# Feed-forward of a hybrid block: squares and rotations bank by bank, the output projection one step later, the token shift as whole rows

## What is computed

```python
h = shift_token(x)                    # second half of each row comes from the row before
q, k, v = split(h @ wqkv)             # 128 -> 3 x 512, 8 heads of 64
q, k = rotary_xpos(l2norm(q) * qs, l2norm(k) * ks)
o = local_attention(q, k, v)          # window 64, keys: own window and the one before
x = x + o @ wo                        # 512 -> 128
h = layernorm(shift_token(x)) * lg + lb
a, g = split(h @ w1 + b1)             # 2 x 341
x = x + (a * gelu(g)) @ w2 + b2
```

## Time and profile before

| | us |
|---|---|
| median of 3 runs | 5035.15 |
| lowest, highest | 5034.42, 5037.8 |
| the profiled execution | 5039.37 |
| its span | 5037.7 |

### The profile page before, as it was taken

How to read it: one execution, slowest core, us unless ns; L and a number is a source line. 1 busy time by engine, 2 the same in 40 slices (tenths; PEclk the granted TensorE clock), 3 DMA queues, 4 the chain that set the end, 5 groups by cost and what they waited for, 6 DMA issues and landing times.

```text
span 5037.7 us, 101534 instructions
## 1 busy us (share of the span) xinstructions
PE 3958.2 (79%) x31924; PEld 2425.0 (48%) x31924; DVE 2871.0 (57%) x5889; ACT 2620.8 (52%) x6422; POOL 1703.7 (34%) x1415
## 2 busy tenths in 40 slices
PE   2999999996688888744666664999999917888886
PEld 1555555553455555522222222777777715555554
DVE  2555555555566676543444443666666656767664
ACT  1555555553566666423333332666666605666664
POOL 0000000000777777523222221111111128777773
PEclk9999999998899999865555555999999959999998
DMA  3222222221101101017999999777777611111111
GB/s 122 78 79 82 78 79 78 84 77 45 44 22 23 24 23 23 16 66 287 382 381 378 381 379 370 260 243 273 242 275 243 227 34 26 23 23 23 23 24 28
DMA packets 373723, 701.02 MB, mean 139 GB/s; under 512 B 53220, under 2 KB 160056, under 8 KB 373608
## 3 DMA queue, kind: packets, MB, share of 16 engines
q1 hardware_dynamic: 329576, 565.25, 32.8%
q0 software_dynamic: 44032, 134.30, 7.3%
HBM read 336.53 MB, written 314.64 MB: 129 GB/s over the span
## 4 chain that ended last, share of the span: by engine, by line
PE 60%; DMA 13%; DVE 7%; issue 7%; POOL 5%; ACT 3%; SPq 1%; DVEq 1%; POOLq 0%; ACTq 0%
DMA rel_k<-b_stage_k 12%; PE ps L332 5%; PE ps L1452 5%; PE ps L340 5%; PE ps L351 5%; PE ps L1461 5%; PE ps L862 4%; PE ps L1443 3%; PE ps L821 3%; PE ps L1472 3%; PE ps L882 2%; PE ps L836 2%; PE ps L847 2%; POOL f_rn L759 2%; PE ps L1344 2%
## 5 line engine op out<-in xcount | busy, mean ns | idle before, releaser
L1368 DVE COPY b_stage_k<-ps 128x640 f32<-128x640 f32 (+2 forms) x512 | 359.3, 722 | 471.1 <-DMA rel_k<-b_stage_k 412.3
L430 ACT ACTIVATE a_p<-a_s,a_min 128x512 f32<-128x512 f32 x512 | 367.1, 718 | 469.6 <-DVE a_min L474 469.6
L1365 ACT ACTIVATE b_stage_q<-ps 128x640 f32<-128x640 f32 (+2 forms) x512 | 316.4, 624 | 506.8 <-PE ps L1347 390.2
L474 DVE CUSTOM_DVE_ANT_0 a_s<-ps,a_table 128x512 f32<-128x512 f32 x512 | 333.5, 689 | 374.4 <-PE ps L332 371.8
L1526 ACT ACTIVATE c_p<-c_s,c_min 128x512 f32<-128x512 f32 x512 | 371.0, 725 | 291.9 <-PE ps L1461 179.8
L1344 PE MATMUL ps<-b_e,b_st_k 48*128 48x512 bf16 (+1 forms) x512 | 305.9, 597 | 263.8 <-DVE b_stage_k L1368 263.8
L1561 DVE CUSTOM_DVE_ANT_0 c_s<-ps,c_rq 128x512 f32<-128x512 f32 x512 | 353.2, 690 | 202.5 <-PE ps L1452 189.8
L188 POOL COPY y<-ln_rows 128x512 f32 x32 | 19.9, 621 | 1305.2 <-DVE ln_rows L180 1305.2
L757 POOL TENSOR_TENSOR f_rot<-f_rc,f_rs 128x1024 f32<-128x1024 f32 x128 | 302.9, 2367 | 354.3 <-DVE f_rs L1017 354.0
L942 ACT ACTIVATE f_p<-f_s,f_min 128x128 f32<-128x128 f32 x1024 | 397.6, 392 | 39.6 <-DVE f_min L1005 35.6
L759 POOL TENSOR_TENSOR f_rn<-f_ss,f_power 128x16 f32<-128x16 f32 x128 | 373.8, 2920 | 14.3 <-DVE f_ss L1026 0.4
(11 more groups left out here) (171 smaller groups left out, 9374.7 us busy)
## 6 DMA issues: line engine op xcount, KB each, us to landing
rel_q<-b_stage_q SPq DMA_DIRECT2D x64, 1280.0 KB, 7.7
rel_k<-b_stage_k SPq DMA_DIRECT2D x64, 1280.0 KB, 7.7
c_rq<-rel_q SPq DMA_DIRECT2D x64, 1024.0 KB, 7.3
c_rk<-rel_k POOLq DMA_DIRECT2D x64, 1024.0 KB, 11.8
a_table<-skew_bias SPq DMA_DIRECT2D x64, 896.0 KB, 4.6
f_vb<-f_v SPq DMA_DIRECT2D x256, 128.0 KB, 2.3
rel_k<-b_stage_k SPq DMA_DIRECT2D x32, 1024.0 KB, 9.4
rel_q<-b_stage_q SPq DMA_DIRECT2D x32, 1024.0 KB, 5.3
```

Source lines behind the costliest of these rows:

```text
L430: nc.scalar.activation(a_p[:, lt % 2, h, :], a_s[:, lt % 2, h, :], ACT.Exp, bias=a_min[:, lt % 2, h:h + 1], scale=-1.0, accum_out=a_sum[:, ...
L1368: moves_b1(dve, 1, lambda out, src: nc.vector.tensor_copy(out, src))
```

## The change

A fifth tile, `d`, four steps behind, enters every `step`. The output projection and the residual add are of `d`, at the start of the next step, in the MIXED bank; `mix_values` waits for that add. `Square` and the rotations go bank by bank with semaphores that count twice and six times a tile. At m=2 the first four exponentials stand behind the copies. At m=3 SP shifts whole rows of `y` (four tiles of 128 numbers, 2 KB a partition) into `f_h`, behind the residual add of `d`, and ahead of its `f_vb` transfers; VectorE then writes the left halves over (they are not shifted), and the statistics follow behind the reciprocal. The bias add on POOL moves from m=0 to m=1. Cut to its core:

```diff
 # sync_ffn
+            if m == 3 and ln is not None:
+                half = slice(DIM // 2, DIM)
+                hold(sp, f_x_mid, upto(d.g))
+                hold(sp, f_hn_ready, upto_b(ln.g - 1, LT))
+                rows = y[:, bass.ts(ln.y, LT), :]
+                sp.dma_start(f_h[1:P, :, :], rows[0:P - 1, :, :]).then_inc(f_shift_loaded, 16)
+                sp.dma_start(f_h[0:1, 1:LT, half], rows[P - 1:P, 0:LT - 1, half]).then_inc(f_shift_loaded, 16)
...
-            if m == 2 and ln is not None:
-                sp.dma_start(f_h[1:P, :, half], rows[0:P - 1, :, :]).then_inc(f_shift_loaded, 16)
...
 # pool_ffn
                 tt(f_rstd[:, :], f_lv[:, :], f_power[:, 0:LT], ALU.pow).then_inc(f_rstd_ready, 1)
-                hold(pool, f_shift_loaded, 32 * (mlp.g + 2))
+            if m == 1 and mlp is not None:
                 hold(pool, f_h_left, upto_b(mlp.g))
...
-            if m == 3 and ln is not None:
-                nc.gpsimd.tensor_copy(f_h[:, :, 0:DIM // 2], y[:, bass.ts(ln.y, LT), 0:DIM // 2]).then_inc(f_h_left, 1)
 # tensor_ffn
-            mm(ps[:, QK, :], h, f_wqkv[:, a.layer, 0:INNER], start=True, stop=True)
+            mm(ps[:, QK, :], h, f_wqkv[:, a.layer, 0:INNER], start=True, stop=True).then_inc(f_qk_full, 1)
 # transpose_qk, for k in (q, k)
+                if a is not None:
+                    pe.wait_ge(f_squared, upto(a.g - 1, 2) + k + 1)
+                    pe.wait_ge(f_turned, upto(a.g - 1, 6) + 3 * k + 3)
 # mix_values
-            pe.wait_ge(f_oT_moved, upto(c.g - 1))
+            pe.wait_ge(f_x_mid, upto(c.g - 1))
 # join_heads(m, d, mlp)
+            if m == 0 and mlp is not None:
+                pe.wait_ge(f_y_done, upto_b(mlp.g - 1))
+            if m == 1 and mlp is not None:
+                pe.wait_ge(f_hnT_moved, upto_b(mlp.g))
+            if m == 2 and mlp is not None:
+                pe.wait_ge(f_gelued, upto_b(mlp.g, 3))
+            if m == 3 and mlp is not None:
+                pe.wait_ge(f_hid_ready, upto_b(mlp.g, 3))
-                last = mm(ps[:, V_BANK, 0:DIM], f_oT[:, i * P:(i + 1) * P], f_wo[:, c.layer, i, :],
+                last = mm(ps[:, MIXED, 0:DIM], f_oT[:, i * P:(i + 1) * P], f_wo[:, d.layer, i, :],
 # new: ahead of turn_normed, chunk 2 of mlp_up and mlp_down
+        def mixed_free(c, d):
+            if c is not None:
+                pe.wait_ge(f_oT_moved, upto(c.g))
+            elif d is not None:
+                pe.wait_ge(f_x_mid, upto(d.g))
 # step of PE: behind project_v, ahead of transpose_probs
+            if d is not None:
+                join_heads(m, d, mlp)
-            if c is not None:
-                join_heads(a, c)
 # scalar_ffn
-                nc.scalar.activation(f_sq[:, :], ps[:, QK:QK + 2, :].rearrange("p b n -> p (b n)"),
-                                     ACT.Square).then_inc(f_squared, 1)
+                for k in range(2):
+                    act.wait_ge(f_qk_full, upto(a.g - 1, 2) + k + 1)
+                    nc.scalar.activation(f_sq[:, k * INNER:(k + 1) * INNER], ps[:, QK + k, :],
+                                         ACT.Square).then_inc(f_squared, 1)
-            if s2 is not None:
+            if s2 is not None and m != 2:
                 exps(s2, 0)
 # behind the copies f_pT, f_qT, f_kT, ahead of f_oT
+            if s2 is not None and m == 2:
+                exps(s2, 0)
 # vector_ffn: turn_heads, for k in (q, k): one rc of 512, two rs of 256
+                dve.wait_ge(f_squared, upto(a.g - 1, 2) + k + 1)
+                tt(rc, heads, cs[:, 0, k, :].unsqueeze(1).broadcast_to([P, HF, DF]), ALU.mult).then_inc(f_turned, 1)
 # statistics: first
+            hold(dve, f_shift_loaded, 32 * (ln.g + 2))
+            nc.vector.tensor_copy(f_h[:, :, 0:DIM // 2], y[:, bass.ts(ln.y, LT), 0:DIM // 2]).then_inc(f_h_left, 1)
 # step of DVE: behind the copy f_pT, ahead of sum_squares
+            if d is not None:
+                dve.wait_ge(f_out_full, upto(d.g))
+                tt(y[:, d.t, :], y[:, d.t, :], ps[:, MIXED, 0:DIM], ALU.add).then_inc(f_x_mid, 1)
 # statistics(ln) now behind the reciprocal
```

More of the change, by code:

```diff
@@ L654, in body @@
             for m in range(LT):
-                step(m, rows(0, m), rows(1, m), rows(2, m), rows(3, m), whole(-1), whole(-2), whole(1))
+                step(m, rows(0, m), rows(1, m), rows(2, m), rows(3, m), rows(4, m), whole(-1), whole(-2), whole(1))
         body(0, 0)
@@ L692, in sync_ffn, with step @@
         sp.wait_ge(f_zeros, F_ZEROS * (call + 1))
-        def step(m, a, b, s2, c, ln, mlp, nxt):
+        def step(m, a, b, s2, c, d, ln, mlp, nxt):
+            if m == 3 and ln is not None:
[5 more added lines that the diff above has]
+                sp.dma_start(f_h[0:1, 1:LT, half], rows[P - 1:P, 0:LT - 1, half]).then_inc(f_shift_loaded, 16)
             if a is not None:
@@ L700, in step @@
                 sp.dma_start(f_vb[0:WINDOW, (m + 1) % LT, :], f_v[WINDOW:P, m, :]).then_inc(f_vb_loaded[m], 16)
-            if m == 2 and ln is not None:
[L702 to L705, removed]
-                sp.dma_start(f_h[1:P, :, half], rows[0:P - 1, :, :]).then_inc(f_shift_loaded, 16)
-                sp.dma_start(f_h[0:1, 1:LT, half], rows[P - 1:P, 0:LT - 1, :]).then_inc(f_shift_loaded, 16)
         ffn_loop(sp, call, step)
@@ L749, in step @@
                 fetch(nxt)
-            if m == 3 and ln is not None:
-                hold(pool, f_x_mid, upto(ln.g * LT + 3))
-                hold(pool, f_hn_ready, upto_b(ln.g - 1, LT))
-                nc.gpsimd.tensor_copy(f_h[:, :, 0:DIM // 2], y[:, bass.ts(ln.y, LT), 0:DIM // 2]).then_inc(f_h_left, 1)
             if a is not None:
-                pool.wait_ge(f_turned, upto(a.g, 3))
+                pool.wait_ge(f_turned, upto(a.g, 6))
                 pool.wait_ge(f_normed, upto(a.g - 1))
@@ L780, in project_qk @@
             if b is not None and s2 is None:
[L781 to L782 removed]
+                pe.wait_ge(f_squared, upto(b.g, 2))
+                pe.wait_ge(f_turned, upto(b.g, 6))
             pe.wait_ge(f_qT_moved, upto(a.g - 2))
             pe.wait_ge(f_kT_moved, upto(a.g - 2))
[L785 removed]
+            mm(ps[:, QK, :], h, f_wqkv[:, a.layer, 0:INNER], start=True, stop=True).then_inc(f_qk_full, 1)
             mm(ps[:, QK + 1, :], h, f_wqkv[:, a.layer, INNER:2 * INNER], start=True, stop=True).then_inc(f_qk_full, 1)
         def project_v(a, h):
[L789 to L791 removed]
+            pe.wait_ge(f_v_moved, upto(a.g - 1))
             mm(ps[:, V_BANK, :], h, f_wqkv[:, a.layer, 2 * INNER:3 * INNER], start=True, stop=True).then_inc(f_v_full, 1)
@@ L826, in transpose_qk @@
         def transpose_qk(a, b):
[L827 to L832, removed]
-            pe.wait_ge(f_normed, upto(b.g))
-            for k, full in enumerate((f_qT_full, f_kT_full)):
+            pe.wait_ge(f_normed, upto(b.g))
+            for k, (full, moved) in enumerate(((f_qT_full, f_qT_moved), (f_kT_full, f_kT_moved))):
+                if a is not None:
+                    pe.wait_ge(f_squared, upto(a.g - 1, 2) + k + 1)
+                    pe.wait_ge(f_turned, upto(a.g - 1, 6) + 3 * k + 3)
+                else:
+                    pe.wait_ge(moved, upto(b.g - 1))
                 for i in range(PAIRS_F):
@@ L1010, in turn_heads @@
             dve.wait_ge(f_rotated, upto(a.g - 1))
[L1011 to L1018, removed]
+            for k in range(2):
+                heads = ps[:, QK + k, :].rearrange("p (h d) -> p h d", d=DF)
+                rc = f_rc[:, k * INNER:(k + 1) * INNER].rearrange("p (h d) -> p h d", d=DF)
+                rs = f_rs[:, k * INNER:(k + 1) * INNER].rearrange("p (h d) -> p h d", d=DF)
+                dve.wait_ge(f_squared, upto(a.g - 1, 2) + k + 1)
+                tt(rc, heads, cs[:, 0, k, :].unsqueeze(1).broadcast_to([P, HF, DF]), ALU.mult).then_inc(f_turned, 1)
+                for h in range(2):
+                    to, src = slice(h * 32, h * 32 + 32), slice((1 - h) * 32, (1 - h) * 32 + 32)
+                    tt(rs[:, :, to], heads[:, :, src],
+                       cs[:, 1, k, to].unsqueeze(1).broadcast_to([P, HF, 32]), ALU.mult).then_inc(f_turned, 1)
         def sum_squares(a):
@@ L1060, in step @@
                 normalize(mlp)
-            if m == 3 and ln is not None:
-                statistics(ln)
             if s2 is not None:
@@ L1066, in step @@
                 nc.vector.reciprocal(f_rsum[:, s2.par, :], f_sum[:, s2.par, :]).then_inc(f_inverted, 1)
-            if c is not None:
-                dve.wait_ge(f_out_full, upto(c.g))
-                tt(y[:, c.t, :], y[:, c.t, :], ps[:, V_BANK, 0:DIM], ALU.add).then_inc(f_x_mid, 1)
+            if m == 3 and ln is not None:
+                statistics(ln)
             if m == 2 and mlp is not None:
```

34 lines of the change are left out of this document (13 added, 21 removed).

## The result

The changed kernel is slower: median 5218.38 us (5216.2 to 5219.62, 4 runs) against 5034.88 (5034.42 to 5037.8), ratio 1.0363, 95% interval 1.0345 to 1.0381. I had forecast 4906, with a range to 4988, and gave "slower" 7 in 100. The page of the profiled execution (5216.2 us) now gives the token shift 7% of the chain that ended last (followed back from the last instruction, at each step to what released it).

The account below looks back on a forecast made before the run. No engine was full, so a cycle of waits was taken as the bound. Intervals of 9.5, 12.0, 13.4 and 13.0 made 47.95 us a batch, saving 109, plus 7 and 14: 130 less, forecast 4906 us, range 4868 to 4988.

Parts of the forecast that it names:

- landing of the shift: At m=3, whole-row data expected at R3+4.5, R3 being the end of m=3's rotations on VectorE; statistics then just covered.
- interval from m=3 to m=0: From the end of m=3's rotations to m=0's: 13.0 us forecast with the low clock charged, 14.8 before.
- third rival: The shift's second transfer keeps its long issue (6.90): batch 2.0 us longer, 5084 us; chance 0.07, shared with other slower mechanisms.
- ends of the calls: Token shift without cover at each call's end gets 7 us shorter: 14 us over two calls.
- seven tiles at the start of each: First seven tiles of each call gain half of 0.97 us a tile: 7 us together, bounds 0 and 14.
- R0 to R1: End of m=0's rotations on VectorE to end of m=1's: 9.5 us forecast, 10.1 before.
- R1 to R2: End of m=1's rotations to end of m=2's: 12.0 us forecast, 12.6 before; square behind Gelu.
- R2 to R3: End of m=2's rotations to end of m=3's: 13.4 us forecast, 14.0 before; reordering gives nothing, the late projection pays.
- The low clock: After m=3, PE's slow clock charged as today: 13.0 us to m=0, against 12.0 at full clock.
- full-clock case: Rival without low clock after m=3: 12.0 us to m=0 in place of 13.0, 4878 us; chance 0.13.
- Squares and rotations by bank: Each tile: VectorE works 0.14 us more, but the first rotation needs only the first bank's squares, about 1.3 earlier.
- The copy held by POOL: Rival at m=3: left-half copy waits for GpSimd's `f_qk`, batch 50.0 us, 4961 us; chance 0.30, shared with half the gain.

Follow-up runs that it names:

- a_split: The changed kernel with the shift of 127 partitions sent as two transfers, of 112 and 15 partitions: 4919.08 us, ratio 0.9767 to the kernel before.
- a_split_exps: The changed kernel with the shift as 112 + 15 partitions and the first four exponentials of m=2 back ahead of the copies: 4894.86 us, ratio 0.9721.
- lv_pool: `a_split_exps` with the addition of eps to the variance (`f_lv`) done by GpSimd, not VectorE: 4883.09 us, ratio 0.9703.
- a_whole: `a_split_exps` with `Square` and rotations over both banks again: 4898.19 us, ratio 0.9732.
- b_bank: `b_split` with squares and rotations bank by bank and nothing else of the change: 5066.78 us, ratio 1.0067.
- b_split: The kernel before the change, with its half-row shift sent as 112 + 15 partitions in place of 127: 5018.9 us, ratio 0.9969.

## Why the prediction was wrong

- **The step that failed is the landing of the shift.** "127 pieces of 2 KB are nearer to `f_vb`'s 64" took the size of a piece for what counts, and the 6.90 of the second issue for the price of 508 pieces. `f_vb` moves 64 partitions, a number with 16 as a divisor; the shift moves 127. R3+4.5 was R3+15, and with it the interval from m=3 to m=0 was 22.6 and not 13.0. My third rival had the place and the sign, but its ground was the issue (it was to decide at 5 us; the issue was 3.9, in five batches 0.7, and the landing late all the same), and its price of 2.0 a batch was 5.6. The sign that it gave was luck. The trace before had what was needed: between 1503 and 1511 the shift's 127 KB ran at 13 GB/s, 0.06 of the 16 engines' time (the window 1503.10 to 1511.00). I looked at issue and landing and not at the DMA share of that window.
- **The rest of the sum held for the batch, not for its two small terms.** With the shift as 112 + 15, which lands about where I had assumed (R3+4.8), a batch of `a_split` takes 48.25 in the first call and 48.78 in the second (13.0, 10.5, 10.6, 13.7, in some batches 14 to 15 for the first) where I had 47.95. In its profiled execution (4932 us; the median is 4919) the batches give 98 of the 109 us that I had. The ends of the calls give 9.5 of 14. The seven tiles at the start of each give nothing of 7: I had put half the gain of a full tile there with no row behind it.
- *R0 to R1 and R1 to R2* were 9.5 and 12.0 in the forecast; by the ends of the rotations after, 9.9 and 11.3 in the batch above, 9.6 and 11.5 at the median. The square did come right behind Gelu, which took 1.84 and not 2.07: before, the third Gelu had started 0.2 late, behind TensorE's product, though I had read the three as without a gap. `f_rot` was 0.75 late in m=1, not 1.3.
- *R2 to R3*: reciprocal at R2+6.5 (6.4 forecast), 13.7 for 13.4. "The reordering itself gives nothing" was too kind to it: it costs 24 us (`a_split_exps`).
- *The low clock* that I charged in m=3 is gone with the shift as 112 + 15 (0.99 over 460 us). So 13.0 from m=3 to m=0 came out right by luck: the charge for the clock, 1.0, was wrong, and two things that I had not charged took its place. `f_lv` was held by GpSimd (without that, in `lv_pool`, it is 12.5), and TensorE's last product let the add to `y` start at R3+6.9 in `lv_pool` and not at the R3+6.4 of my full-clock case.
- *Squares and rotations by bank*: of no effect on the sum (`a_whole`), and a loss of 48 us without the late projection (`b_bank`). The gain comes from the output projection's new place and the order that goes with it: from `b_split`'s 5019 to `a_whole`'s 4898. No run takes the projection's place apart from the later shift and statistics.
- *The copy held by POOL* was a rival at its right size (15.0 from m=3 to m=0), in 9 of 32 batches of `a_split` instead of all.

## What to carry to other kernels

Before a transfer is judged by its bytes or pieces, look at the DMA share of the window in which it is alone: 0.06 means one engine of 16, and then the number of partitions on the slowest dimension is the first thing to change (112 + 15 in place of 127). A transfer that is badly spread costs nothing while it starts early; moving it later by a step can put most of its length on the path (10.0 of 13.8 us here), so its length must be measured and explained first, not inferred from a relative. And a shorter wait can cost more than it gives where it lengthens another one before TensorE (2.04 to 2.50 in `b_bank`): look at the granted clock of the next tiles.

## What the runs showed of the hardware

- SBUF to SBUF, at the share of one DMA engine (0.06 to 0.07): 127 rows of 2 KB land 13.8 us after the issue (25 GB/s), 113 rows 12.9, and 508 pieces of 256 bytes 10.4 (13 GB/s); as 112 + 15 the 127 rows land in 3.6, issue of three transfers included.
- SyncE's next issue behind such a transfer is often long too: 3.8 to 4.3 behind 127 rows (but 0.7 in 5 of 32), 0.9 to 3.3 behind 113, 6.8 to 7.0 behind the 508 pieces, 0.9 behind 112 in all 32.
- Two kinds of VectorE operation with one SBUF input are held until GpSimd's 1024-wide operation ends: a copy, 1.85 for 0.29, and the addition of a constant to four numbers, 1.03 for 0.17. The statistics (L1040), with one SBUF input too, take 0.87 beside `f_qk` as they do alone. Beside GpSimd's small power neither `f_hn` (1.10) nor the copy (0.29) was held.
- After waits of TensorE of 2.50 (`b_bank`, for `f_p`) and 7.37 us the granted clock was at 1.2 GHz in the next stretch; after the wait of 2.04 for `f_p` in `b_split` it was not. The length of the wait alone does not decide it: `b_bank` has waits of 1.84 and then 0.60 ahead of its transposes of `f_qk` (1512.53, 1513.79), and the clock was at 1.2 GHz from 1513.9 to 1517.3.
